# Inverse root of the tokens' variance: Newton's steps on VectorE instead of GpSimd's power

## What is computed

```
xn = (x - mean(x)) / sqrt(var(x) + 1e-5)                # per token, over 512 features
q, k, v = xn Wq' + bq, xn Wk' + bk, xn Wv' + bv
context = (elu(q)+1) * cumsum((elu(k)+1) * v) * 32**-0.5
s = context Wo' + bo
h = fwht(xn * SU_ug) / 64 ; up, gate = h W_up', h W_gate'  (scaled)
h = fwht(silu(gate) * up * SU_dp) / 64
g = silu(h W_down' * scale)
out = x + s * g
```

## Time and profile before

| what | us |
| --- | --- |
| median of 3 runs | 1354.0 |
| the profiled execution, its own time | 1353.09 |
| its span, first to last instruction | 1351.3 |
| TensorE busy with matmuls | 1312.9 (97%) |
| VectorE busy | 1011.6 (75%) |
| ScalarE busy | 452.1 (33%) |
| GpSimd busy | 52.2 (4%) |
| mean granted TensorE clock | 0.994 |

### The profile page before, as it was taken

The page is one execution under the profiler, slowest core; times in us unless marked ns, Lnnn a source line. Parts: engine busy times, 40 slices in busy tenths (PEclk is TensorE's granted clock), DMA queues, the critical chain, the costliest instruction groups (busy, mean ns, idle before and its releaser), DMA issues. The chain is left out here.

```text
span 1351.3 us, 16205 instructions
## 1 busy us (share of the span) xinstructions
PE 1312.9 (97%) x6164; PEld 612.6 (45%) x6164; DVE 1011.6 (75%) x1618; ACT 452.1 (33%) x651; POOL 52.2 (4%) x85
## 2 busy tenths in 40 slices
PE   3998999999999999999999999999999999999998
PEld 2544454544454444444444444444444444444443
DVE  5699999987847998778734898778743998787333
ACT  4844464452123443332112433332111443332000
POOL 0022210001100000000000000000000000000000
PEclk8989999999999999999999999999999999999999
DMA  9414555567665323325244332334243423333230
GB/s 369 203 63 164 187 215 189 188 219 274 215 214 172 128 94 125 123 98 185 94 156 140 141 113 106 125 125 149 105 166 113 170 108 125 112 107 125 94 125 32
DMA packets 48270, 201.24 MB, mean 149 GB/s; under 512 B 5312, under 2 KB 5568, under 8 KB 32704
## 3 DMA queue, kind: packets, MB, share of 16 engines
q1 hardware_dynamic: 41568, 177.13, 36.7%
q0 software_dynamic: 6624, 23.07, 4.7%
HBM read 155.09 MB, written 45.09 MB: 148 GB/s over the span
## 5 line engine op out<-in xcount | busy, mean ns | idle before, releaser
L1415 PE MATMUL bank<-xops,ring 128*128 128x512 f16 x2772 | 601.1, 379 | 2.9 <-DVE work L882 2.4
L1415 PEld LDWEIGHTS bank<-xops,ring 128*128 128x128 f16 x2772 | 269.8, 98 | 333.7 <-DVE work L882 10.9
L882 DVE TENSOR_TENSOR work<-bank,work 128x512 f32<-128x512 f32 x462 | 305.0, 684 | 92.2 <-PE bank L1415 85.4
L1481 PE MATMUL bank<-ring,h_all 128*128 128x512 f16 x1536 | 334.0, 379 | 0.5 <-DVE gate_g L1149 0.5
L1321 PE MATMUL bank<-xops,ring 128*128 128x512 f16 x1056 | 239.1, 384 | 6.7 <-DVE ring L980 6.3
L1481 PEld LDWEIGHTS bank<-ring,h_all 128*128 128x128 f16 x1536 | 150.1, 98 | 180.7 <-DVE gate_g L1149 1.0
L1321 PEld LDWEIGHTS bank<-xops,ring 128*128 128x128 f16 x1056 | 103.9, 99 | 137.9 <-issue 15.9
L671 ACT ACTIVATE h_all<-work 128x512 f16<-128x512 f32 x128 | 80.2, 627 | 211.1 <-DVE work L921 211.1
L1149 DVE TENSOR_TENSOR gate_g<-bank,row 128x512 f32<-128x512 f32 x32 | 21.4, 688 | 106.7 <-PE bank L1481 106.2
L930 DVE TENSOR_TENSOR h_all<-work,h_all 128x512 f16<-128x512 f32 x128 | 87.1, 683 | 0.4
L664 ACT ACTIVATE work<-work,gate_out 128x512 f32<-128x512 f32 x96 | 66.4, 715 | 54.3 <-DVE work L882 54.3
(11 more groups left out here) (146 smaller groups left out, 888.0 us busy)
## 6 DMA issues: line engine op xcount, KB each, us to landing
ring<-scr_g SPq DMA_DIRECT2D x66, 1024.0 KB, 4.8
ring<-scr_d SPq DMA_DIRECT2D x32, 1024.0 KB, 4.8
scr_g<-ring SPq DMA_DIRECT2D x22, 512.0 KB, 3.8
scr_g<-ring POOLq DMA_DIRECT2D x22, 512.0 KB, 3.7
h_all<-in_ug_t SPq DMA_DIRECT2D x8, 1024.0 KB, 22.1
ring<-scr_f POOLq DMA_DIRECT2D x16, 512.0 KB, 4.4
x_res<-in_x SPq DMA_DIRECT2D x32, 256.0 KB, 3.7
out<-x_res SPq DMA_DIRECT2D x32, 256.0 KB, 6.7
```

The costliest lines, as they stand in the source:

```text
L882: dve.tensor_tensor(tile(g, to), bank[product][:, :], tile(g, other), ALU.add).then_inc(summed, 1)
L1415: mm = pe.matmul(bank[n][:, :], weight_of(slot, s, b, kk), xops[:, kk, xs, c, :], start=(a == 0), stop=(a == 5))
L1481: mm = pe.matmul(bank[D_BANK[t]][:, :], at[:, s, cols], w[:, :, ws, :], start=(a == 0 and b == 0 and n == 0), stop=(a == KB - 1 and b == K ...
```

## The change

GpSimd's power goes, in all four pairs, with the tile of exponents and both semaphores. On VectorE `var_eps` is now followed by a wait for its own end, and `normalise` first calls `inverse_root`: a first guess from the bits (half of the exponent, subtracted from a constant; two instructions) and three of Newton's steps of three instructions each, r <- r * (1.5 - 0.5 * v * r * r), each instruction waited for by the next. The multiplication by 256 stays.

```diff
@@ GpSimd
-            pool.memset(minus_half[:, :], -0.5).then_inc(halves_set, 1)
-            pool.wait_ge(halves_set, 1)
-
-            def rstd_of(p):
-                pool.wait_ge(var_ready, p + 1)
-                pool.tensor_tensor(rstd[:, :], var_eps[:, :], minus_half[:, :], ALU.pow).then_inc(rstd_ready, 1)
...
-            rstd_of(0)
...
-                if n == S_EARLY + 1:
-                    rstd_of(1)
             for p in range(1, PAIRS):
-                if p > 1:
-                    rstd_of(p)
                 ctx_max_of(p)
@@ VectorE
-                dve.tensor_scalar(var_eps[:, :], mean_var[:, :, 1], EPS, None, ALU.add).then_inc(var_ready, 1)
+                prep.after(dve.tensor_scalar(var_eps[:, :], mean_var[:, :, 1], EPS, None, ALU.add))
+
+            def inverse_root():
+
+                prep.after(dve.tensor_scalar(newton[:, :].bitcast(I32), var_eps[:, :].bitcast(I32), 1, None,
+                                             ALU.logical_shift_right))
+                prep.after(dve.tensor_scalar(rstd[:, :].bitcast(I32), newton[:, :].bitcast(I32), -1.0,
+                                             float(INVERSE_ROOT_BITS), ALU.mult, ALU.add))
+                for _ in range(NEWTON_STEPS):
+                    prep.after(dve.scalar_tensor_tensor(newton[:, :], rstd[:, :], -0.5, rstd[:, :], ALU.mult, ALU.mult))
+                    prep.after(dve.tensor_tensor(newton[:, :], newton[:, :], var_eps[:, :], ALU.mult))
+                    prep.after(dve.scalar_tensor_tensor(rstd[:, :], newton[:, :], 1.5, rstd[:, :], ALU.add, ALU.mult))
+                prep.after(dve.tensor_scalar(rstd[:, :], rstd[:, :], X_SCALE, None, ALU.mult))
 
             def normalise(p):
-                dve.wait_ge(rstd_ready, p + 1)
-                prep.after(dve.tensor_scalar(rstd[:, :], rstd[:, :], X_SCALE, None, ALU.mult))
+                inverse_root()
```

More of the change, by code:

```diff
@@ L39 @@
 ROOT_BITS = 127 << 22
+INVERSE_ROOT_BITS, NEWTON_STEPS = 0x5F3759DF, 3
 MARGIN = 1.02
@@ L168, in build @@
         norms = sb("norms", [P, 2 * NI])
-        minus_half = sb("minus_half", [P, 2 * TB])
         ones = sb("ones", [P, 1], BF16)
@@ L183, in build @@
         var_eps, rstd = sb("var_eps", [P, 2 * TB]), sb("rstd", [P, 2 * TB])
+        newton = sb("newton", [P, 2 * TB])
         ctx_max, ctx_max_all = sb("ctx_max", [P, 9]), sb("ctx_max_all", [P, 1])
@@ L206, in build @@
         prep_step = sem("prep_step")
-        halves_set, ones_set = sem("halves_set"), sem("ones_set")
+        ones_set = sem("ones_set")
         attn_squared, attn_bounded, attn_scaled = sem("attn_squared"), sem("attn_bounded"), sem("attn_scaled")
@@ L219, in build @@
         o_hi, o_made = sem("o_hi"), sem("o_made")
-        var_ready, rstd_ready, xn_ready, xp_done = sem("var_ready"), sem("rstd_ready"), sem("xn_ready"), sem("xp_done")
+        xn_ready, xp_done = sem("xn_ready"), sem("xp_done")
         b12_copied, x_hi, t_made = sem("b12_copied"), sem("x_hi"), sem("t_made")
```

## The result

The changed kernel takes 1360.88 us (median of 6 executions, 1358.61 to 1364.67), the kernel before 1354.03 us (6 executions, 1353.53 to 1355.05). The ratio is 1.0049, with a 95% interval of 1.0038 to 1.0061: slower by 6.6 us, 5.1 to 8.3. The forecast was 1361.6. The profiled execution was the fastest of the six, 1358.61 us with a span of 1356.7; that is 5.4 us more span than before. One of the 63 later executions of the kernel before took 2832.47 us and is in none of the ratios and spreads.

A forecast was written before the change was run, and what follows sets the result against it. TensorE, 97% busy, was taken to bound the kernel, so changes elsewhere act only through its waits. Start -0.4, first join -0.2, later joins +4.8 and clock +3.4 sum to +7.6 us: median 1361.6, range 1357.2 to 1365.0.

The forecast's parts named there:

- Price of the chain: On VectorE, per pair: 11 new chained instructions take 2.29 us, the wait behind var_eps 0.12; together 2.41 us, bounds 2.2 to 3.0.
- Second and third join: Joins of pairs 1-2 and 2-3: nothing covers the chain, TensorE's waits become 3.75 and 2.4 us; +4.8 us together.
- The clock: Behind the new waits at the two later joins: one half-clock fall each at 1.7 us, +3.4 us, bounds 0 and 6.2.
- Both falls: Main case: TensorE's clock falls at both later joins, +7.6 us in all, 1361.6 us; chance 0.45.
- the three prices: Losses at half clock about TensorE's existing waits of 6.3, 2.6 and 4.6 us: 1.6, 3.1 and 1.7 us.
- dearer: Rival at the later joins: chain 3.0 us and two falls at about 2.4 us each, +10.2, 1364.2 us; chance 0.07.
- faster: Rival in pair 0: VectorE and GpSimd run 1.9 us ahead, TensorE's waits shrink, clock stays up; -3.7, 1350.3 us; chance 0.04.
- First join: Join of pairs 0 and 1: chain ends 0.24 us earlier than the power, TensorE's gate wait shrinks; -0.2 us, bounds -0.4, +0.4.
- The start: Pair 0's beginning: without the power K's maximum comes by 15 us, first weights and TensorE's first group 1.9 us earlier.
- The net of -0.4 us: At the start: of 1.9 us gained only 0.4 get past the wait for the first store; bounds +0.8 and -1.9.
- the forecast wait of 1.5 us: Before TensorE's sums near 50.7 us: most of the earlier start becomes a new wait of about 1.5 us.
- one fall only: Rival at the later joins: the clock falls only at the second join, +5.9 us, 1359.9; chance 0.27.

The follow-up runs named there:

- the repeat: The changed kernel run again, unaltered, on the same chip: 1361.84 us, ratio 1.0050 to the kernel before.
- pairs 1 to 3 alone: Against the kernel before: Newton's steps in pairs 1 to 3 only, GpSimd's power kept for pair 0; 1361.35 us, ratio 1.0059.
- discarded matmuls: Against the changed kernel: matmuls with thrown-away results added in TensorE's waits before the transposes of pairs 2 and 3; 1358.09 us, ratio 1.0028 to the kernel before.
- late down loads: Against the changed kernel: SyncE's two loads of the down weights issued behind the first store, not ahead; 1358.49 us, ratio 1.0036 to the kernel before.
- pair 0 alone: Against the kernel before: Newton's steps in pair 0 only, GpSimd's power kept for pairs 1 to 3; 1353.47 us, ratio 0.9992.
- early normalise: Against the changed kernel: normalise(p + 1) put ahead of the context's eight splits at the two later joins; 1350.93 us, ratio 0.9982 to the kernel before.
- early normalise by the power: Against the kernel before: GpSimd's power kept in all pairs, normalise(p + 1) put ahead of the context's splits; 1352.46 us, ratio 0.9984.

## Why the prediction was right

The time, 1360.88 and 1361.84 against 1361.6, is right, and so is the mechanism at the two later joins, which make nearly all of it. That it came within 1 us is partly luck: the two profiled executions of the changed kernel have 5.4 and 8.3 us more span than the one before, on both sides of the forecast 7.6, and differ by one fall of the clock and by what happened in pair 0.

- **Price of the chain.** 11 steps were put at 2.29 us and took 2.21: the two-tensor steps have the pitch of the one-tensor ones, 0.20 and not 0.21. The wait behind `var_eps` cost 0.12 as forecast (0.20 instead of 0.08). The semaphore does cost something here. The Trainium skill's sentence, by which it would have cost nothing (VectorE: DVE Perf Modes, The DRAIN you can't avoid), rests on a measurement of eight copies; the trace of these 128x8 instructions doesn't agree with it.
- **Second and third join.** New waits of 3.75 and 2.4 us were forecast; 3.58 and 2.36 (3.64 and 2.39 in the repeat) were found. The experiment with pairs 1 to 3 alone puts the whole loss there. With the clock held up by discarded matmuls the joins cost 4.8 us more than before (977.6 against 972.8), the 4.8 of the sum.
- **The clock.** One fall at each join, 3.4 us together, was taken. Both falls cost 3.1 us in the traces (980.7 against 977.6). The fall after the longer wait is in all four traces of kernels with a wait near 3.6 us (changed, repeat, pairs 1 to 3 alone, late down loads), the fall after the shorter one in two of them. So the price fits, and the doubt between one fall and two was not a doubt between cases: both occur, from one execution to the next. How often each does, and so what the median holds, isn't known. "Both falls" was too sure in that sense.
- **A price that was none.** Of the three prices the 3.1 us for the fall about the wait of 2.6 us (L1356) is not lost at the end. After that same wait, 2.64 or 2.65 us, the granted clock fell in eight of the thirteen profiled executions and stayed at 1.00 in five (pair 0 alone, early normalise, late down loads, early normalise by the power, repeat). From its end to the end of the next wait, for VectorE's L987, it is 25.1 to 25.4 us in all thirteen: TensorE at full clock only waits longer. The forecast took 1.7 and was not touched; the rivals "dearer" and "faster" counted on the 3.1.
- **First join.** 0.24 us earlier relative to the last sums was forecast; from `s_low` to the normalised blocks' start it took 3.56 us (355.80 to 359.36) in place of 3.87, 0.31 less. TensorE's wait of 0.5 us went in the profiled execution and was 0.24 in the repeat.
- **The start.** K's maximum near 15 and TensorE's first group near 25.2 were forecast; 14.4 and 24.78 came. The net of -0.4 us was the weak term. In the changed kernel's profile 1.05 us got past the sums (50.01 against 51.06), for two reasons that the forecast did not have. The store landed earlier as well (46.77 against 47.68), which I had ruled out but for a bound. And the clock stood at half for longer behind the shorter wait on the first weights, so that the first 24 matmuls took 8.25 us, not 6.93, and ended 1.05 us earlier and not 2.4; that is why the forecast wait of 1.5 us wasn't there. In the repeat (6.92 us for the 24) and in pair 0 alone the wait was there, 2.9 and 1.1 us. With the first join, -0.6 us was forecast up to the transposes; -0.9 and, in the repeat, +0.4 were found. What the start is worth at the end is between 0 and 2 us (the experiment on pair 0), and a further lead is lost at the first join, which I had not named: ScalarE waits there for a store of the weight sums.

One rival was partly true: "one fall only" describes some executions. "Faster" failed at the point that I had named for it: the waits of 2.6 and 4.6 us did not shrink.

## What to carry to other kernels

Price a move between engines by what the receiving engine is doing at that moment: GpSimd's 1.7 us were hidden behind VectorE's splits, while 2.3 us of tiny chained instructions (0.20 us each, whatever they compute) stood at the end of the one stretch that TensorE waits for. Before trading the operation, try the order: putting the awaited result ahead of work that nobody needs yet made the question of engine irrelevant behind the first join. And count a lengthened wait of TensorE dearer than its length where the clock falls after it, here by some 1.6 us a fall, unless TensorE waits for another engine soon after: in pair 0 the fall cost nothing. When executions spread, compare the length of a stretch in the traces, not only the medians.

## What the runs showed of the hardware

- Feeding TensorE with matmuls of no use during a wait of 3.6 us and one of 2.4 us kept the granted clock at 2.4 GHz in the profile and took about 3 us off the kernel.
- A wait of about 2.4 us was followed by the half clock (1.2 GHz) in one execution (3.3 us at 0.50) and not in another of the same kernel; a wait of 2.65 us in pair 0 was followed by it in eight of thirteen traces. After the waits of 1.34 to 1.37 us and 1.84 us at the second join it did not fall.
- The changed kernel's times spread over 6 to 8 us, those of the kernel before over 1.5 us in the first six and up to 4.0 us in the later series. The falls at the joins are 3.3 us of that at most; what makes the rest, in pair 0, wasn't tested. The landing of the first store moves by 2.1 us there: in four executions of the same program up to that point (changed, repeat, discarded matmuls, early normalise) ScalarE's third weights start at 46.77 to 48.84.
- With GpSimd going from the power to the maximum over partitions 9.66 us passed before the next instruction, and 9.84 and, in the kernel with the power in pairs 1 to 3 only, 10.49 us on the way to the power. With the power gone from pair 0 the first maximum waits for nothing but ScalarE's squares (14.37 instead of 23.15).
